# First attention of a four-part model: a second set of scores with keys on partitions, row maxima as rows of the contraction, fp32 probabilities used as they leave PSUM

## What is computed

```
Q = (x @ Wq.T).reshape(b, h, t, d)      # b=4, h=16, t=512, d=16
K, V likewise
scores = einsum('bhqd,bhkd->bhqk', Q, K);  scores = where(causal, -inf, scores)
weights = softmax(scores / sqrt(d), axis=-1)
ctx = einsum('bhqk,bhkd->bhqd', weights, V).transpose(0, 2, 1, 3).reshape(b, t, e)
x = layernorm(x + ctx @ Wp.T + bp)
```

## Time and profile before

| | us |
|---|---|
| median of 3 runs (1041.6, 1045.97, 1046.72) | 1045.97 |
| the profiled execution | 1045.61 |
| its span from first to last instruction | 1043.8 |
| PE busy | 909.4 (87%) |
| DVE busy | 822.5 (79%) |
| ACT busy | 629.8 (60%) |
| POOL busy | 373.0 (36%) |

### The profile page before, as it was taken

How to read it: one execution, slowest core, us unless ns; L and a number is a source line. 1 busy time by engine, 2 the same in 40 slices (tenths; PEclk the granted TensorE clock), 3 DMA queues, 4 the chain that set the end, 5 groups by cost and what they waited for, 6 DMA issues and landing times.

```text
span 1043.8 us, 23337 instructions
## 1 busy us (share of the span) xinstructions
PE 909.4 (87%) x8624; PEld 627.8 (60%) x8745; DVE 822.5 (79%) x2400; ACT 629.8 (60%) x1560; POOL 373.0 (36%) x605
## 2 busy tenths in 40 slices
PE   6778778877767988998899999999999999798796
PEld 3667666766653443434566566666666667586454
DVE  6999998989985787675899988888888888523555
ACT  5999998989862434343666655555555555423443
POOL 4333443430422455444333333333333333200354
PEclk9999999999988999999999999999999999999999
DMA  7202121200000000000466655555565555400011
GB/s 265 63 22 62 42 62 42 56 9 2 2 2 1 1 1 1 1 1 1 77 124 115 123 99 99 99 98 97 100 102 102 102 102 99 91 1 1 1 41 41
DMA packets 174626, 61.41 MB, mean 59 GB/s; under 512 B 169248, under 2 KB 170800, under 8 KB 174384
## 3 DMA queue, kind: packets, MB, share of 16 engines
q1 hardware_dynamic: 174512, 59.90, 28.3%
HBM read 15.83 MB, written 2.10 MB: 17 GB/s over the span
## 4 chain that ended last, share of the span: by engine, by line
PE 50%; DVE 30%; ACT 7%; issue 5%; POOL 5%; DMA 4%; SPq 0%; POOLq 0%; DVEq 0%; ACTq 0%
PE bank L349 12%; PE bank L350 12%; PE bank L348 11%; DVE s_sb L1130 7%; DVE pt_lo L1087 4%; DVE scr L1087 4%; DVE scr L1117 3%; DMA pt_lo<-w_lo 3%; PE bank L663 3%; PE bank L665 3%; PE bank L664 3%; ACT scr L798 2%; ACT s_sb L845 2%; POOL scr L1592 2%; DVE w_lo L1148 2%
## 5 line engine op out<-in xcount | busy, mean ns | idle before, releaser
L1130 DVE CUSTOM_DVE_ANT_0 s_sb<-bank,consts 128x512 f32<-128x512 f32 (+3 forms) x512 | 227.8, 481 | 23.3 <-PE bank L350 15.0
L847 ACT ACTIVATE s_sb<-s_sb,nm 128x512 f32<-128x512 f32 (+3 forms) x256 | 141.5, 553 | 103.7 <-DVE nm L1130 102.4
L348 PE MATMUL bank<-w_hi,scr 128*128 128x256 bf16 (+1 forms) x566 | 169.9, 300 | 16.7 <-DVE scr L1087 13.8
L349 PE MATMUL bank<-w_lo,scr 128*128 128x256 bf16 (+1 forms) x575 | 173.5, 302 | 1.9 <-issue 1.8
L350 PE MATMUL bank<-w_hi,scr 128*128 128x256 bf16 (+1 forms) x572 | 172.0, 301 | 0.1
L798 ACT ACTIVATE scr<-bank 128x256 bf16<-128x256 f32 (+4 forms) x256 | 119.8, 486 | 75.2 <-PE bank L665 43.3
L845 ACT ACTIVATE s_sb<-s_sb,nm 128x512 f32<-128x512 f32 (+3 forms) x256 | 141.0, 583 | 13.3 <-DVE nm L1130 13.2
L1087 DVE TENSOR_TENSOR pt_lo<-bank,pt_hi 128x512 bf16<-128x512 f32 (+1 forms) x192 | 108.5, 592 | 8.1 <-ACT pt_hi L798 8.1
L1622 POOL TENSOR_SCALAR wqkv_hi<-s_sb,rr 128x512 bf16<-128x512 f32 (+3 forms) x128 | 65.6, 532 | 137.6 <-DVE rr L1154 137.6
L1087 DVE TENSOR_TENSOR scr<-bank,scr 128x256 bf16<-128x256 f32 (+1 forms) x160 | 80.5, 524 | 39.6 <-ACT scr L798 39.4
L1622 POOL TENSOR_SCALAR w_hi<-s_sb,rr 128x512 bf16<-128x512 f32 (+3 forms) x128 | 65.6, 532 | 105.2 <-DVE rr L1154 105.2
(11 more groups left out here) (160 smaller groups left out, 2393.7 us busy)
## 6 DMA issues: line engine op xcount, KB each, us to landing
scr<-wall_in SPq DMA_DIRECT2D x19, 512.0 KB, 3.7
x_tok<-x_tok_in SPq DMA_DIRECT2D x1, 2048.0 KB, 10.6
scr<-x_t_in SPq DMA_DIRECT2D x3, 512.0 KB, 9.3
out<-x_tok SPq DMA_DIRECT2D x3, 512.0 KB, 3.1
scr<-wqkv_in SPq DMA_DIRECT2D x2, 384.0 KB, 3.9
pt_hi<-w_hi SPq DMA_TRANSPOSE x32, 3.3
pt_lo<-w_lo SPq DMA_TRANSPOSE x32, 3.4
pt_hi<-wqkv_hi SPq DMA_TRANSPOSE x32, 3.4
```

The costliest lines, as they stand in the source:

```text
L348: pe.matmul(out, l_hi, r_hi, start=start, stop=False, skip_group_check=check)
L349: pe.matmul(out, l_hi, r_lo, start=False, stop=False, skip_group_check=check)
L847: last = act.activation(at, at, ACT.Exp, bias=nm[:, j % 2, qt:qt + 1], scale=-1.0, accum_out=rs[:, j % 2, qt:qt + 1])
L1130: last = dve.tensor_tensor_reduce(s_sb[j % 2][:, S_OFF[qt]:S_OFF[qt] + w], bank[turn][:, col:col + w], mask[:, 512 - w:512], -scale, HUGE, ...
```

## The change

Heads are now worked in pairs, one "slot" for each pair (32 slots, `NP`), with six slots before the first (`FIRST_SLOT = -6`). A group has two slots; the pair is heads j and j+2 of the group, because 64-row halves of the tokens give them.

- `q_tok` and `k_tok` are double-buffered and have 64 slots for each block: 48 as before, and rows 48 to 50 of k are ones, those of q zero. The values are no part of k any more.
- `l0_stack` makes 32 transposes of 64x64 for q and 32 for k (two array quarters, one for each half of the tokens), into bank 6. ACT copies all of q out (`l0_q_stack`), DVE all of k (`l0_k_stack`), 128x1024 each. Both stacks have three buffers.
- `l0_scores` makes the same scores as before, for both heads of a pair, alternating between rows 0-63 and 64-127 of the array, into banks 0 to 2. `l0_maxima` writes the masked scores back over the scores in PSUM; only the maxima are used.
- POOL splits the maxima in three bf16 parts (`l0_split_maxima`, four instructions of 128x8 in a chain). `l0_row_maxima` (PE) makes in bank 7 the queries' stack (one 512-column product with the identity) plus the maxima turned into rows 48 to 50 (four 128-column products); ACT copies it to `q_max`, 128x512 bf16.
- `l0_turned_scores` makes the scores again with keys on partitions in banks 3 to 5: 10 blocks for each head as four products of 512, 384, 128 and 256 columns, whose contraction now subtracts the maximum, and before each the mask, by two small products of 64 and 128 columns with a `future` matrix of large values.
- `l0_exponentials` (ACT) reads 512, 512 and 256 columns of PSUM for each head and writes fp32 probabilities to SBUF. They have keys on partitions already.
- `l0_context` multiplies them with fp32 values: 10 fp32 matmuls of 17 columns for each head, in place of 10 fp32 transposes and 30 bf16 matmuls.
- The values go from PSUM to SBUF (ACT, 128x256 fp32), by DMA to a DRAM tensor and by a second DMA back with positions on partitions in 64-byte pieces (`v_out`, `v_back`, both on SP's queue).
- POOL splits 29 of the 38 weight halves, over 27 slots; ACT makes the high half of the nine odd chunks (`weights_high`). The bias additions and small weights of POOL come in slots 27 to 31, and the early steps in slots 30 and 31 (`EARLY_AT`).
- Gone are the turning of values (4 matmuls for each head), the fp32 transposes, the two-part copies of the probabilities, and first attention's exponentials in SBUF.

The core of the diff:

```diff
+q_tok = [... .rearrange("p (c s) -> p c s", s=ROWS) for i in range(2)]      # ROWS = 64
+q_stack = [scr[:, 8192 + 512 * i:8704 + 512 * i].bitcast(BF16) for i in range(3)]
+v_dram = nc.dram_tensor("v_by_token", (NB * TOK, E), F32, kind="Internal").ap()
...
# SP
+            def v_out(g):
+                sp.wait_ge(a["vt"], g + 1)
+                sp.dma_start(v_dram[g * P:(g + 1) * P, :], v_tok[g % 2]).then_inc(v_wr[g % 2], 16)
+            def v_back(g):
+                hold(sp, a["pv"], 2 * g - 2)
+                sp.wait_ge(v_wr[g % 2], 16 * (g // 2 + 1))
+                sp.dma_start(
+                    v_pos[g % 2][:, :, :, 0:D0].rearrange("p u k d -> p (u k) d"),
+                    v_dram[g * P:(g + 1) * P, :].rearrange("(n t) (c d) -> (t c) n d", t=8, d=D0)
+                ).then_inc(v_ld[g % 2], 16)
...
# PE
+                for ch in range(HEADS):
+                    for h in range(2):
+                        last = pe.transpose(out[half(h), ch * ROWS:(ch + 1) * ROWS], tok[half(h), ch, :],
+                                            ident_b[half(h), half(h)])
...
+            def l0_row_maxima(p):
+                g, j = divmod(p, 2)
+                if g + 2 < NT:
+                    pe.wait_ge(*((a["vt"], g + 3) if j == 1 else (a["plo"], 2 * g + 6)))
+                pe.wait_ge(a["spl"], p + 1)
+                pe.matmul(bank[7][:, :], ident_b[:, :], q_stack[g % 3][:, ds(j * TOK, TOK)], start=True, stop=False,
+                          skip_group_check=True)
+                for qt in range(TT):
+                    last = pe.matmul(bank[7][:, qt * P:(qt + 1) * P], m_cols[p % 2][:, qt, :], ident_b[:, :],
+                                     start=False, stop=True, skip_group_check=True)
+                last.then_inc(a["nm"], 1)
+            def l0_turned_scores(p, chunk):
...
+                out = [bank[3 + (6 * p + 2 * chunk + h) % 3] for h in range(2)]
+                for i, (kt, col) in enumerate(K_CHUNKS[chunk]):
+                    for part, w in enumerate((ROWS, P)):
+                        for h in range(2):
+                            if i == 0 and part == 0:
+                                hold(pe, a["exp"], 6 * p + 2 * chunk + h - 2)
+                            turned = h != part
+                            pe.matmul(out[h][:, col:col + w], (ident_b, ident_s)[turned][half(h), :],
+                                      (future, future_s)[turned][half(h), 0:w], start=(i == 0 and part == 0),
+                                      stop=False, skip_group_check=True)
+                    w = TOK - kt * P
+                    for h in range(2):
+                        last = pe.matmul(out[h][:, col:col + w], k_stack[g % 3][half(h), ds(j * TOK + kt * P, P)],
+                                         q_max[p % 2][half(h), kt * P:TOK], start=False, stop=True,
+                                         skip_group_check=True)
...
+            def l0_context(p):
+                g, j = divmod(p, 2)
+                pe.wait_ge(a["exp"], 6 * p + 6)
+                pe.wait_ge(v_ld[g % 2], 16 * (g // 2 + 1))
+                hold(pe, a["vc"], p)
+                pe.wait_ge(*((a["stq"], min(g + 4, NT)) if j == 1 else (a["stk"], min(g + 3, NT))))
+                for h in range(2):
+                    for qt in range(TT):
+                        at = (h * TT + qt) * VC
+                        for kt in range(qt + 1):
+                            col = prob_col(h, kt) + (qt - kt) * P
+                            last = pe.matmul(bank[6][:, at:at + VC], probs[p % 2][:, col:col + P],
+                                             v_pos[g % 2][:, 2 * h + j, kt, :], start=(kt == 0), stop=(kt == qt),
+                                             skip_group_check=True)
+                last.then_inc(a["pv"], 1)
+            def l0_slot(p):
+                g, j = divmod(p, 2)
+                for chunk in range(3):
+                    if 0 <= p + 2 < NP:
+                        l0_scores(p + 2, chunk)
+                    if 0 <= p < NP:
+                        l0_turned_scores(p, chunk)
+                    if chunk == 0 and 0 <= p + 1 < NP:
+                        l0_row_maxima(p + 1)
+                    if chunk == 1 and 0 <= g + 2 < NT:
+                        l0_stack(g + 2, j)
+                    if chunk == 2 and 0 <= g + 3 < NT:
+                        (l0_project, l0_values)[j](g + 3)
...
+                if 0 <= p - 1 < NP:
+                    l0_context(p - 1)
# ACT
+            def l0_slot(p):
+                for chunk in range(3):
+                    if 0 <= p < NP:
+                        l0_exponentials(p, chunk)
+                    if chunk == 0 and 0 <= p - 2 < NP:
+                        l0_context(p - 2)
+                    if chunk == 0 and 0 <= p + 1 < NP:
+                        l0_query_maxima(p + 1)
+                    if chunk == 1 and j == 0 and 0 <= g + 2 < NT:
+                        l0_q_stack(g + 2)
+                    if chunk == 2 and 0 <= g + 3 < NT:
+                        (l0_parts_high, l0_values)[j](g + 3)
...
```

More of the change, by code:

```diff
@@ L77, with weight_halves @@
 TB = 7
-C_ALL = 7
+C_ALL = 10
 WARM = 9
+Z_ALL = 2
+BIAS_SLOTS = range(27, 31)
+X_SLOTS = {-3: 1, 6: 2, 14: 3}
+WEIGHT_SLOTS = range(-1, 26)
+POOL_HALVES = [(n, part) for n in range(NCH) for part in range(2) if part == 1 or n % 2 == 0]
+def weight_halves(p):
+    if p not in WEIGHT_SLOTS:
+        return []
+    i, n, all_ = p - WEIGHT_SLOTS[0], len(WEIGHT_SLOTS), len(POOL_HALVES)
+    return POOL_HALVES[all_ * i // n:all_ * (i + 1) // n]
 def tail_steps():
@@ new lines, in l0_stack, with l0_scores @@
+                out = bank[6][:, :].bitcast(BF16)
+                for ch in range(HEADS):
+                    for h in range(2):
+                        last = pe.transpose(out[half(h), ch * ROWS:(ch + 1) * ROWS], tok[half(h), ch, :],
+                                            ident_b[half(h), half(h)])
+                last.then_inc(a[("tq", "tk")[which]], 1)
+            def l0_scores(p, chunk):
+                g, j = divmod(p, 2)
+                if chunk == 0:
+                    pe.wait_ge(a["stk"], g + 1)
+                for i, (qt, col) in enumerate(S_CHUNKS[chunk]):
+                    w = (qt + 1) * P
+                    for h in range(2):
+                        n = 6 * p + 2 * chunk + h
+                        if i == 0:
+                            hold(pe, a["max"], n - 2)
+                        last = pe.matmul(bank[n % 3][:, col:col + w],
+                                         q_stack[g % 3][half(h), ds(j * TOK + qt * P, P)],
+                                         k_stack[g % 3][half(h), ds(j * TOK, w)], start=True, stop=True)
+                        if i == len(S_CHUNKS[chunk]) - 1:
+                            last.then_inc(a["s"], 1)
@@ new lines, in l0_query_maxima, with l0_exponentials @@
+            def l0_query_maxima(p):
+                hold(act, a["st"], 6 * (p - 1))
+                act.wait_ge(a["nm"], p + 1)
+                copy(q_max[p % 2], bank[7][:, :]).then_inc(a["qt"], 1)
+            def l0_exponentials(p, chunk):
+                if chunk == 0:
+                    hold(act, a["pv"], p - 1)
+                for h in range(2):
+                    n = 6 * p + 2 * chunk + h
+                    act.wait_ge(a["st"], n + 1)
+                    act.activation(probs[p % 2][:, ds(prob_col(h, chunk), T_LEN[chunk])],
+                                   bank[3 + n % 3][:, 0:T_LEN[chunk]], ACT.Exp, scale=D0 ** -0.5
+                                   ).then_inc(a["exp"], 1)
@@ new lines, in l0_maxima @@
+            def l0_maxima(p, chunk):
+                if chunk == 0:
+                    hold(dve, a["spl"], p - 1)
+                for h in range(2):
+                    n = 6 * p + 2 * chunk + h
+                    dve.wait_ge(a["s"], n + 1)
+                    for qt, col in S_CHUNKS[chunk]:
+                        w = (qt + 1) * P
+                        rows = bank[n % 3][:, col:col + w]
+                        last = dve.tensor_tensor_reduce(rows, rows, mask[:, 512 - w:512], -1.0, HUGE, ALU.add, ALU.min,
+                                                        nm0[:, p % 2, h, qt:qt + 1])
+                    last.then_inc(a["max"], 1)
@@ L1508, in _ @@
             pool.memset(ones_b[:, :], 1.0).then_inc(c_ready, 1)
-            pool.memset(scr[:, 8192:12288], 0.0).then_inc(z_ready, 1)
+            for i in range(2):
+                last = pool.memset(k_tok[i][:, :, M_ROW:M_ROW + 3], 1.0)
+            last.then_inc(z_ready, 1)
             pool.memset(one_f[:, :], 1.0).then_inc(c_ready, 1)
```

546 lines of the change are left out of this document (244 added, 302 removed).

## The result

| | before | after |
|---|---|---|
| median, us | 1045.82 (4 runs, 1041.6 to 1046.72) | 1312.28 (4 runs, 1308.28 to 1314.05) |
| span of the profiled execution | 1043.8 | 1310.8 |
| mean granted clock | 0.975 | 0.825 |

The changed kernel is slower by a ratio of 1.2552 [1.2508, 1.2597], 240 us beyond the upper end of the range given.

A forecast was written before the change was run, and what follows sets the result against it. DVE and ACT, tied together, were taken to bound the kernel. Start 27.5 us, 30 slots of 8.1 (243) less 4, last slots 13, early steps 11 and last context 3.5 gave 294 against 312: 1028 us, range 985 to 1072.

The forecast's parts named there:

- slots of 8.1: First attention: each slot takes 5.1 us up to the context product plus 3.0 for it, against 8.8 a pair before.
- DVE and ACT leave the bound: Engines that set the rate before: DVE falls to 4.9 us and ACT to 5.0 us a slot, below PE.
- PE's part of the slot: PE's scores, turned scores, row maxima, projections and transposes: 4.1 us a slot, plus 0.3 for tiling changes.
- rival 2: Score products on the two halves of the array's rows do not overlap: PE has 1.2 to 1.4 us more a slot; chance 0.15.
- On ACT that is ... to 4.9 us. On DVE ... `k_stack` to 4.6: Order of copies within a slot: stack copies end at 4.9 and 4.6 us, so the context begins at about 5.1.
- 20 x 0.15 = 3.0: Context product on PE: 20 fp32 matmuls of 17 columns at 0.15 us each, 3.0 us a slot.
- rival 1: Each fp32 context product takes two full 0.108 us spacings: 4.3 us a slot, slot 9.4, 1067 us; chance 0.20.
- The start: Work before slot 0, with both stacks copied one after the other: first turned score near 27.5 us.
- The values' way by DRAM: Values' write to DRAM and read back: 14 us available, 2048 pieces should need 5 to 8 us.
- rival 4: The values' DMA lands late and each second slot waits 1 to 2 us: 1043 to 1055 us; chance 0.05.
- POOL's work "hidden under 8.1": POOL's 2.1 us weight half and some 2 us of small work, 4.5 a slot in all, costed at nothing.
- The mechanism that I ranked third: fp32 product costs 2.2 us or less and waits overlap it: slots of 6.2 to 7 us, 971 to 995; chance 0.17.

The follow-up runs named there:

- e7: e3 with ACT's weight high halves made one slot earlier and SP's chunk loads issued ahead of the values' transfers: 971.14 us, ratio 0.9293.
- e1: The changed kernel with both stack copies writing neighbouring columns side by side instead of every 16th: 1133.18 us, ratio 1.0852.
- e9: e1, fp32 products kept, with the same weight-half and load reordering as e7: 1132.34 us, ratio 1.0867.
- e12: e7 with every bf16 context product issued eight times, 160 products of 17 columns a slot: 1079.65 us, ratio 1.0324.
- e3: The changed kernel with e1's copy order and e2's bf16 context product, low parts left out: 1012.49 us, ratio 0.9683.
- e2: The changed kernel with the context product in bf16, low parts of probabilities and values left out, copies unchanged: 1109.35 us (single run).
- e6: e1 with the context as three bf16 products, low parts written by DVE, plus e7's reordering: 1096.38 us, ratio 1.0512.
- e8: e6 with POOL making the low part of 1024 of 2560 columns and ACT copying the k stack: 1080.12 us, ratio 1.0342.

## Why the prediction was wrong

It forecast 1028 us from slots of 8.1; the slots were 16.9. By its own steps:

- **DVE and ACT leave the bound: right.** DVE is busy 229 of the 575.3 us from 18.7 to 594 us, 40% where 60 was forecast (of a shorter slot) and 92 stood before; exponentials out of PSUM 0.594 us, forecast 0.60. DVE's maxima into PSUM cost more than the nothing I took: the four widths took 0.04, 0.04, 0.09 and 0.05 us longer than in the earlier trace rows (0.715 against 0.676 for 512), and the read of the accumulator 0.141 against 0.078; for two heads that is 2 x 0.22 + 8 x 0.063 = 0.95 us a slot, beyond my upper bound of 0.5. DVE waited 132 us for PE, so it had room. Only the two stack copies, below, stand in PE's path.
- **PE's part of the slot: right.** PE works 5.4 us ahead of the gap at a mean clock of 0.66; in e7, at full clock, that part takes 4.5 us, where 4.4 was forecast. The halves do run side by side, rival 2 falls: the timeline of e7 shows both heads' 512-column scores within the 0.39 us that one takes alone, and 32 transposes in 0.69 us, below my 1.1 and below even the bound of 0.8:

```profile
151.22 0.39 PE L483 MATMUL bank<-scr 64*128 64x512 bf16 x2
...
153.77 0.69 PE L468 MATMUL bank<-ident_b,scr 64*64 64x64 bf16 x32
```

  Here the Trainium skill (TensorEngine Tiling, Key Properties), by which different tiles run in parallel, agrees with the trace.
- **"On ACT that is ... to 4.9 us. On DVE ... `k_stack` to 4.6": the first step that failed.** I took the copies' durations from the earlier trace rows by their size and engine. The diff shows the new write order, every 16th column, and I did not price it. The context began at 8.9 us of the slot (220.4 to 229.3), not 5.1; by e1 the order was worth 179 us. With e1's copies of 1.03 and 1.22 us the forecast's step holds: there one context ends at 217.3 us and the next begins at 222.4, 5.1 later.
- **"20 x 0.15 = 3.0": the second, in size.** The product takes two records, 0.22 us at full clock, 4.5 a slot: rival 1's price (0.216) and past its turning point, given as 0.19 (by its own slot of 8.7, less 5.1, it is 0.18). The reason against rival 1, that the transposes' 0.108 us holds their 128 columns, was wrong: with 17 columns a record takes 0.11 all the same. The Trainium skill (FP8 and Floating Point Precision, TensorE Precision Notes) gives "4 passes"; the trace has two records for each product, and 160 bf16 products in 4.17 us are one every 0.025 us, so one fp32 product takes the time of nine small ones.
- **The clock: missing from the sum.** I took the 0.99 of the earlier trace rows for granted in a stretch with another mix. It had 0.65 (100 to 300 us). With e1's copies that is some 40 of the 53 us by which e9 lies over e12, and more with copies of 4.5 us, whose gaps the falls of the clock follow. Rival 1 as I worked it out gives 1067; with the 53 and 5 for a first turned score at 32.7 us in place of 27.5 it gives 1125, an estimate, and e1 measured 1133.
- **The start: 11.7 us late.** Copies of 4.5 us stand in it one after the other; with those of e1 it is 5.2 late, which my own working of the start has to answer for.
- **The values' way by DRAM: right.** The read back lands in 3.1 us (I had 5 to 8), the write in 1.8; rival 4 falls.
- **POOL's work "hidden under 8.1": right only while PE is slow.** With 5.8 us slots its place in the order cost 41 us (e3 to e7).

The mechanism that I ranked third, slots of 6.2 to 7 us and 971 to 995 us, is what the change's order gives once copies and product are cheap: e7, at 971, beats both kernels, with the low parts of probabilities and values left out. Among versions that keep them the kernel before stays the fastest one measured.

## What to carry over

Price a moved copy by its access pattern on both sides, not by its columns: the diff's `rearrange` cost 179 us where the whole change was to gain 18. When a change puts a new type of product on PE, look for it in any trace you have, and leave room for the clock: here it depended on what ran as well as on idle time. And read a wait's worth beside its engine's rank: the same reordering gave 41 us in one kernel and none in another.

## What the runs showed of the hardware

- Writes of 2 bytes at a step of 16 elements (32 bytes) take 4.46 us for 1024 columns on ACT and DVE alike, 4.4 ns a column; the same values read with a step out of PSUM and written side by side take 1.03 and 1.22 us. The Trainium skill (SBUF — State Buffer, Door 1: The DMA port swizzle) names lines of 16 bytes, within which bf16 may be strided up to 8 elements for free, with a penalty beyond; the trace agrees for the step of 16. No other step was run.
- An fp32 product of 128x128 by 17 columns is two records, one every 0.11 us at 2.4 GHz and every 0.21 at 1.2. In slots of such products the clock falls though PE hardly pauses: 0.78 over 60 to 300 us in e9, with PE busy 99%, against 0.86 in e12 with 160 bf16 products of the same shape in place of 20, and 0.93 in e7 with 20 bf16 ones.
- Gaps cost the clock too. In the changed kernel its falls lie in or right behind PE's waits of 2.4 to 3.8 us for the copies; e2, with such waits and bf16 products, has 0.72, e3 without them 0.87, and e7, without most of the waits for POOL too, 0.93.
- DVE and POOL slow each other. The same subtraction of 272 columns on DVE takes 0.52 us in e6 and 1.93 in e8, where POOL makes its large low part at that point; and POOL's cast of eight columns takes 0.85 us in e6, where DVE starts its low parts at that point, and 0.22 in e7, where there are none. Both rows of DVE at 60 to 400 us, first e6:

```profile
L1175 DVE TENSOR_TENSOR scr<-scr 128x272 bf16<-128x272 f32 x15 | 7.7, 516 | 0.0
```

  then e8:

```profile
L1185 DVE TENSOR_TENSOR scr<-scr 128x272 bf16<-128x272 f32 x14 | 27.0, 1931 | 0.0
```

  What the two engines share there was not tested apart.
- DVE's instruction that reads its accumulator takes 141 ns where the operation before it wrote to PSUM, and 78 where it wrote to SBUF.
